# A bias put into the accumulation banks by ScalarE, and the last layer norm taken tile by tile

## The reference, cut to what matters

```python
x = layernorm(x + attention(x))          # linear attention, 32 heads of 128, gated, output projection
base   = x @ base_W.T + base_b           # 512 -> 512, the bias of 512 is what the change moves
probs  = softmax(x @ router_W.T + router_b)       # 15 routes
topk_p, topk_i = top_k(probs, 8)                  # 8 of 15; routes mapped to 8 experts
w      = sum of topk_p by expert                  # 8 weights a token
h      = x @ A.T                                  # 8 experts x rank 16
out    = base + (h * w) @ B * 2.0
x = layernorm(x + out)
```

## Time and profile before

| | us |
|---|---|
| median of 3 runs | 1011.59 (1011.27 to 1011.64) |
| the profiled execution | 1010.33 |
| its span | 1008.5 |
| TensorE busy | 994.7 (99%) |
| VectorE busy | 765.4 (76%) |
| ScalarE busy | 662.9 (66%) |
| GpSimd busy | 344.3 (34%) |

### The profile page before, as it was taken

How to read it: one execution, slowest core, us unless ns; L and a number is a source line. 1 busy time by engine, 2 the same in 40 slices (tenths; PEclk the granted TensorE clock), 3 DMA queues, 4 the chain that set the end, 5 groups by cost and what they waited for, 6 DMA issues and landing times.

```text
span 1008.5 us, 15712 instructions
## 1 busy us (share of the span) xinstructions
PE 994.7 (99%) x5620; PEld 873.8 (87%) x5620; DVE 765.4 (76%) x1102; ACT 662.9 (66%) x1108; POOL 344.3 (34%) x329
## 2 busy tenths in 40 slices
PE   8999999999999999999999999999999999999996
PEld 6878998889888898889988898888988899888886
DVE  6777875787857966778757878578677787699885
ACT  6577754787467764677647874677647786477644
POOL 1453232441443223432323414342224323321462
PEclk9999999999999999999999999999999999999999
DMA  6111121111211111111111102111111121110402
GB/s 209 34 59 57 51 70 43 50 50 30 71 43 50 50 56 49 60 50 58 53 54 58 50 30 71 42 50 51 50 50 63 40 68 51 42 51 22 147 22 84
DMA packets 48813, 57.77 MB, mean 57 GB/s; under 512 B 4320, under 2 KB 40032, under 8 KB 48736
## 3 DMA queue, kind: packets, MB, share of 16 engines
q1 hardware_dynamic: 48736, 56.77, 18.1%
HBM read 54.65 MB, written 2.10 MB: 56 GB/s over the span
## 4 chain that ended last, share of the span: by engine, by line
PE 92%; DVE 2%; ACT 2%; issue 1%; POOL 1%; DMA 1%; SPq 0%; POOLq 0%; ACTq 0%; DVEq 0%
PE ps L1834 20%; PE ps L1835 19%; PE ps L1836 19%; PE ps L1828 10%; PE ps L1829 9%; PE ps L1830 9%; PE ps L1926 2%; PE ps L1941 1%; PE ps L1928 1%; PE ps L1943 1%; DMA acc<-xt 1%; DMA stage<-stream 0%; DVE xl L1030 0%; POOL rstd L1726 0%; ACT wh L388 0%
## 5 line engine op out<-in xcount | busy, mean ns | idle before, releaser
L1834 PE MATMUL ps<-xh,wh 128*128 128x512 f32 x658 | 261.9, 398 | 0.6 <-ACT stg L436 0.6
L1835 PE MATMUL ps<-xl,wh 128*128 128x512 f32 x658 | 257.2, 391 | 0.0
L1836 PE MATMUL ps<-xh,wl 128*128 128x512 f32 x658 | 256.1, 389 | 0.0
L1743 POOL TENSOR_TENSOR stage<-stage 128x512 f32<-128x512 f32 x61 | 85.6, 1403 | 323.6 <-DMA stage<-stream 323.3
L1763 POOL TENSOR_TENSOR sqacc<-sqacc,sq 128x512 f32<-128x512 f32 x64 | 92.4, 1444 | 279.0 <-ACT sq L547 279.0
L1030 DVE TENSOR_TENSOR wl<-stage,wh 128x1024 fp32r<-128x1024 f32 (+2 forms) x145 | 155.7, 1084 | 32.6 <-ACT wh L388 32.5
L388 ACT ACTIVATE wh<-stage 128x1024 fp32r<-128x1024 f32 (+2 forms) x145 | 122.1, 855 | 55.8 <-PE ps L1830 33.7
L1836 PEld LDWEIGHTS ps<-xh,wl 128*128 128x128 f32 x658 | 123.6, 188 | 26.6
L1834 PEld LDWEIGHTS ps<-xh,wh 128*128 128x128 f32 x658 | 123.6, 188 | 24.1 <-issue 1.0
L1835 PEld LDWEIGHTS ps<-xl,wh 128*128 128x128 f32 x658 | 123.9, 188 | 22.0
L1834 PE MATMUL ps<-wh,xh 128*128 128x256 f32 (+1 forms) x416 | 121.0, 291 | 0.0
(11 more groups left out here) (201 smaller groups left out, 2193.7 us busy)
## 6 DMA issues: line engine op xcount, KB each, us to landing
stage<-stream SPq DMA_DIRECT2D x61, 384.0 KB, 3.3
stage<-stream SPq DMA_DIRECT2D x42, 256.0 KB, 2.9
stage<-stream SPq DMA_DIRECT2D x63, 128.0 KB, 2.1
dec<-decay SPq DMA_DIRECT2D x32, 192.0 KB, 2.3
acc<-xt SPq DMA_DIRECT2D x8, 256.0 KB, 6.2
v<-x SPq DMA_DIRECT2D x8, 256.0 KB, 5.6
out<-acc SPq DMA_DIRECT2D x8, 256.0 KB, 2.0
sfull<-lora_router SPq DMA_DIRECT2D x1, 512.0 KB, 4.7
```

The source lines that it names most:

```text
L1743: nc.gpsimd.tensor_tensor(stage[:, s, 1:5:3, :], stage[:, s, 0:6:5, :], stage[:, s, 7:8, :].broadcast_to([P, 2, U]), ALU.add).then_inc(t_p ...
L1834: nc.tensor.matmul(dst, wt[0], mv_[0], start=start, stop=False, skip_group_check=True)
L1835: nc.tensor.matmul(dst, wt[0], mv_[1], start=False, stop=False, skip_group_check=True)
L1836: return nc.tensor.matmul(dst, wt[1], mv_[0], start=False, stop=stop, skip_group_check=True)
```

## The change

The bias is put into seven of the eight accumulation banks by a copy on ScalarE, before the base product, whose matmuls all add onto it and are all of 400 columns. Tile 5, whose bank 6 is in use until late, keeps its opening matmul of 512 columns, and its bias is added to `acc` by GpSimd as before, once, after the weighted values of the first four tiles. The load of the bias is issued ahead of the last weights. The first columns are added right after the router's logits. The opening matmul of the second tile in each bank of the router product no longer sets the start flag. The second layer norm: tiles 5, 6 and 7 have statistics from VectorE and are normalized by it; tiles 0 to 4 go through ScalarE as before, each after the next one's square, and GpSimd makes their roots one tile at a time.

```diff
+STATS = 5
+OPENED = 5
@@ SP
-            rows_load(TAIL_LOAD + 4, 1)
             sp.wait_ge(sq_added, 2 * HEADS)
             sp.dma_start(bb, base_b.partition_broadcast(P)).then_inc(bias_in, 16)
+            rows_load(TAIL_LOAD + 4, 1)
             for t in range(TT):
-                if t < TT - 1:
+                if t < STATS:
                     sp.wait_ge(out_ready, t + 1)
                 else:
-                    sp.wait_ge(last_ready, 1)
+                    sp.wait_ge(last_ready, t - STATS + 1)
@@ ScalarE
+            def bias(t):
+                if t < 4:
+                    act.wait_ge(x1_done, t + 5)
+                elif t == 4:
+                    act.wait_ge(hw_done, 2)
+                    act.wait_ge(columns_added, 2)
+                else:
+                    act.wait_ge(ffn_read, t - 5)
+                act.wait_ge(bias_in, 16)
+                nc.scalar.activation(ps[:, FFN_BANK[t], :], bb, ACT.Copy).then_inc(bias_set, 1)
...
             variance(6)
+            bias(0)
+            bias(1)
             normalize(6, ln1_done)
             variance(7)
+            bias(2)
             transposed(5)
             normalize(7, ln1_done)
+            bias(3)
             exponent(0)
             transposed(6)
             transposed(7)
             lora_weights_hi()
+            bias(4)
             lora_transposed(0)
             exponent(1)
+            bias(6)
+            variance(TT)
             lora_transposed(1)
-            for t in range(4):
-                variance(TT + t)
-            for t in range(4):
-                normalize(TT + t, out_ready)
-            for t in range(4, 7):
-                variance(TT + t)
-            for t in range(4, 7):
-                normalize(TT + t, out_ready)
+            bias(7)
+            variance(TT + 1)
+            normalize(TT, out_ready)
+            variance(TT + 2)
+            normalize(TT + 1, out_ready)
+            variance(TT + 3)
+            normalize(TT + 2, out_ready)
+            variance(TT + 4)
+            normalize(TT + 3, out_ready)
+            normalize(TT + 4, out_ready)
@@ VectorE
             def first_columns(f):
-                dve.wait_ge(bias_added, HG * f + HG)
+                dve.wait_ge(tr_done, HG * f + HG)
+                if f == OPENED // HG:
+                    dve.wait_ge(bias_added, 1)
...
+            def statistics(t):
+                dve.wait_ge(ffn_read, t + 1)
+                link(nc.vector.bn_stats(stat[:, t - STATS, :], acc[:, t, :]))
+                nc.vector.bn_aggr(mv[:, t - STATS, :], stat[:, t - STATS, :]).then_inc(last_stats, 1)
+
+            def second_norm(t):
+                dve.wait_ge(last_rstd, 1 if t < TT - 1 else 2)
+                nc.vector.tensor_scalar(acc[:, t, :], acc[:, t, :], mv[:, t - STATS, 0:1], rstd[:, TT + t:TT + t + 1],
+                                        ALU.subtract, ALU.mult).then_inc(last_ready, 1)
...
             router_logits(0)
+            first_columns(0)
             transposed(6)
             router_top(0)
             transposed(7)
             router_weights(0)
-            first_columns(0)
...
             router_logits(1)
+            first_columns(1)
             lora_transposed(0)
             router_top(1)
             router_weights(1)
-            first_columns(1)
+            for t in range(4):
+                second_residual(t)
+                if t:
+                    second_centre(t - 1)
+            second_centre(3)
             lora_transposed(1)
+            second_residual(4)
+            second_residual(5)
+            second_centre(4)
+            statistics(5)
+            second_residual(6)
+            statistics(6)
+            second_residual(7)
+            statistics(7)
+            second_norm(5)
+            second_norm(6)
+            second_norm(7)
@@ GpSimd
-            for t in range(TT):
-                add_bias(t)
-            for n, m in ((8, 2), (10, 2), (12, 2), (14, 1)):
-                means(n, m)
-                affine(n, m)
+            def root(t, n):
+                i = t - STATS
+                pool.wait_ge(last_stats, i + n)
+                link(nc.gpsimd.tensor_scalar(mv[:, i:i + n, 1], mv[:, i:i + n, 1], EPS, None, ALU.add))
+                nc.gpsimd.tensor_tensor(rstd[:, TT + t:TT + t + n], mv[:, i:i + n, 1], half_power[:, 0:n], ALU.pow)\
+                    .then_inc(last_rstd, 1)
+            pool.wait_ge(bias_in, 16)
+            pool.wait_ge(tr_done, OPENED + 1)
+            pool.wait_ge(hw_done, 2)
+            nc.gpsimd.tensor_tensor(acc[:, OPENED, :], acc[:, OPENED, :], bb, ALU.add).then_inc(bias_added, 1)
+            for t in range(4):
+                means(TT + t)
+                affine(TT + t)
+            means(TT + 4)
+            affine(TT + 4)
+            root(5, 2)
+            root(7, 1)
@@ TensorE
             def base(t):
...
-                if t < 4:
-                    pe.wait_ge(x1_done, t + 5)
-                elif t == 4:
-                    pe.wait_ge(columns_added, 2)
-                elif t == 5:
+                if t == OPENED:
                     pe.wait_ge(ht_lo, 1)
                 else:
-                    pe.wait_ge(ffn_read, t - 5)
+                    pe.wait_ge(bias_set, t + 1 if t < OPENED else t)
                 for k in range(KT):
...
-                    if k == 0:
+                    if t == OPENED and k == 0:
                         mm3_first(...)
-                    else:
-                        mm3_onto(...)
+                        continue
+                    mm3_onto(ps[:, FFN_BANK[t], XB:W], ..., False, False)
```

More of the change, by code:

```diff
@@ L139, in build @@
         total = sb("total", [P, 2 * TT])
-        stat = sb("stat", [P, 6])
-        mv = sb("mv", [P, 2])
+        stat = sb("stat", [P, TT - STATS, 6])
+        mv = sb("mv", [P, TT - STATS, 2])
         centre = sb("centre", [P, 2 * TT])
@@ L210, in build @@
         acc_scaled, last_added, x1_done, var_done = sem("acc_scaled"), sem("last_added"), sem("x1_done"), sem("var_done")
-        affine_done, ln1_done, bias_added = sem("affine_done"), sem("ln1_done"), sem("bias_added")
+        affine_done, ln1_done, bias_set, bias_added = sem("affine_done"), sem("ln1_done"), sem("bias_set"), sem("bias_added")
         pool_step = sem("pool_step")
@@ L1611, in second_residual @@
                 dve.wait_ge(ffn_done, t + 1)
-                dve.wait_ge(bias_added, t + 1)
                 dve.wait_ge(columns_added, t // 2 + 1)
-                if t == TT - 1:
+                if t >= STATS:
                     nc.vector.tensor_tensor(acc[:, t, :], acc[:, t, :], ps[:, FFN_BANK[t], :], ALU.add)\
@@ L1675, in _ @@
             router_weights(1)
-            first_columns(1)
-            second_residual(0)
-            second_residual(1)
-            second_centre(0)
-            second_centre(1)
-            lora_transposed(1)
-            second_residual(2)
-            second_residual(3)
-            second_centre(2)
-            second_centre(3)
-            for t in range(4, TT - 1):
-                second_residual(t)
-                if t > 4:
-                    second_centre(t - 1)
-            second_centre(TT - 2)
-            second_residual(TT - 1)
-            dve.wait_ge(ffn_read, TT)
-            link(nc.vector.bn_stats(stat[:, :], acc[:, TT - 1, :]))
-            nc.vector.bn_aggr(mv[:, :], stat[:, :]).then_inc(last_stats, 1)
-            dve.wait_ge(last_rstd, 1)
-            nc.vector.tensor_scalar(acc[:, TT - 1, :], acc[:, TT - 1, :], mv[:, 0:1], rstd[:, 2 * TT - 1:2 * TT],
-                                    ALU.subtract, ALU.mult).then_inc(last_ready, 1)
+            for t in range(4):
[3 more added lines that the diff above has]
+            second_centre(3)
+            lora_transposed(1)
+            second_residual(4)
[9 more added lines that the diff above has]
+            second_norm(7)
         @block.gpsimd
@@ L1728, in affine @@
                     .then_inc(affine_done, m)
-            def add_bias(t):
-                pool.wait_ge(bias_in, 16)
-                pool.wait_ge(tr_done, t + 1)
-                nc.gpsimd.tensor_tensor(acc[:, t, :], acc[:, t, :], bb, ALU.add).then_inc(bias_added, 1)
             parts = [0]
@@ L1812, in _ @@
                 affine(t)
-            for t in range(TT):
-                add_bias(t)
-            for n, m in ((8, 2), (10, 2), (12, 2), (14, 1)):
-                means(n, m)
-                affine(n, m)
-            pool.wait_ge(last_stats, 1)
-            link(nc.gpsimd.tensor_scalar(mv[:, 1:2], mv[:, 1:2], EPS, None, ALU.add))
-            nc.gpsimd.tensor_tensor(rstd[:, 2 * TT - 1:2 * TT], mv[:, 1:2], half_power[:, 0:1], ALU.pow)\
-                .then_inc(last_rstd, 1)
+            def root(t, n):
[15 more added lines that the diff above has]
+            root(7, 1)
         @block.tensor
@@ L2220, in router_and_lora @@
                     for k in range(KT):
```

(12 more changed lines are left out.)

## The result

The changed kernel took 1006.38 us (median of 6 runs, 1005.61 to 1008.05), the kernel before beside it 1011.43 (6 runs, 1009.66 to 1012.4): a ratio of 0.9954, interval 0.9941 to 0.9967. The profiled execution took 1006.4 with a span of 1004.6.

What follows compares the result with a forecast made beforehand. TensorE is busy 99%, so only its waits and the tail count: -1.09 (gap), -0.3 (matmuls), -2.5 (tail), +0.2 (stores), +0.3 (hold) make -3.4; 1011.59 - 3.4 = 1008.2 us, range 1007.2 to 1009.8.

Steps and rivals of the forecast that it cites:

- The gap: TensorE's wait on VectorE before the first four tiles' LoRA transposes, at 982.36: closes whole, -1.09 us.
- Narrower matmuls: TensorE: seven of eight base products start with 400 columns instead of 512, taken as -0.3 us.
- The copies: ScalarE's seven bias copies into PSUM: 0.6 us each (bounds 0.5 and 0.8), no delay to TensorE.
- The thinnest slack: Tile 6's bias copy, done by 990.4, before TensorE reaches base 6 at 991.3: 0.9 us of slack.
- The bias load: Issued ahead of the last weight load, behind the LoRA-router load: taken as costing 0, bounds 0 and 0.9 us.
- Fair sharing: If loads share DMA bandwidth fairly, the earlier bias load delays ScalarE's start after the weights by 0.9 us.
- Rival B: The bias load delays the weights at 945.8 and so TensorE's first transposes: up to +0.9, 1009.1 us; chance 0.1.
- The tail: From tile 7's residual to its normalization: 2.7 us instead of 5.20, so -2.5.
- rival A: VectorE's normalizations of tiles 5 and 6 hold GpSimd's last root: last normalization 0.65 later, 1008.5 us; chance 0.2.
- C: GpSimd's additions aren't what holds the router's long operations; the gap mostly stays: gain 2.3, 1009.3 us; chance 0.1.
- D: ScalarE becomes TensorE's gate, base products wait for its copies: +1.5, 1013.1 us; chance 0.04.
- the stores: At the end, the last three outputs follow 0.55 apart while a store needs 0.65: +0.2 us, bounds 0 and 0.4.

Runs made afterwards that it cites:

- r2_hold: The changed kernel plus eight extra GpSimd additions of 512 columns, into memory nobody reads, beside the first router pass: 1008.3 us, 0.9972 of the kernel before.
- r2_wide: The changed kernel with all base products beginning with 512 columns again, zero weights in the 112: 1007.43 us, 0.9964 of the kernel before.
- r2_scalar_56: The changed kernel with tiles 5 and 6 normalized by ScalarE instead of VectorE: 1007.88 us, 0.9969 of the kernel before.
- r3_split: The changed kernel with tile 5 alone normalized by ScalarE, tiles 6 and 7 by VectorE: 1007.0 us, stretch from the mark to the end 66.47.

## Why the time fell below the range

**What held, by the prediction's own steps.**
- *The gap* closed whole. The sum starts at 972.45 (972.63 forecast), and the wait is gone. The hold by GpSimd's additions is shown both ways: taken away by the change, brought back by `r2_hold`.
- *Narrower matmuls:* 0.34 against 0.3, by `r2_wide`. With the gap, -1.41 against -1.39.
- *The copies* take 0.58 to 0.60 (0.6 forecast) and no base product waits. The thinnest slack was put at 0.9, at base 6: its bank was copied at 989.66 to 990.26, TensorE starts it at 991.15.
- *The bias load* costs 0. The Trainium skill (DMA: Bandwidth & Descriptors, on HWDGE ordering) has each DMA engine take one ring's descriptors in order, and for the weights, two loads ahead, the traces agree: they landed in 2.9 to 3.1 us with the bias load behind them and in 2.9 to 3.3 without. Fair sharing, the other end of the bound, is not what these rows show. For the 512 KB load directly ahead they don't decide: 4.3 to 5.8 us in ten traces with it, 4.3 to 4.9 in seven without. Rival B had TensorE's first transposes waiting for just these weights. They show no idle time ahead of them in either kernel, and in the changed one 0.64 of a delay would have been hidden.
- *The tail:* 2.98, where 2.7 and half a hold of 0.65 made 3.0. So rival A is half true: the hold is real, 0.19 on the first operation and 0.14 on the root, 0.35 on the path by `r2_scalar_56`. The first operation ends just after tile 5's normalization (1000.11 + 0.55 = 1000.66, and 1000.70), as A had it, and so in `r3_split` (1000.24 + 0.54 = 1000.78, and 1000.86). The root doesn't wait for tile 6's end at 1001.08 to begin its 0.58, which would give 1001.66: it ends at 1001.50. The two pages of the Trainium skill that spoke for A (GPSIMD Engine Reference, Key points; VectorE: DVE Perf Modes, Mode 2×_2P) agree as to the kind of instruction that contends; the size is the trace's.
- *Rivals B, C and D* fell. With the bias load late, ScalarE's queue did cost 1.47, but at tile 7's low half and not at the base products, as D had it.

**What failed.** First, a term: the stores. +0.2 was put for the last three leaving 0.55 apart, -0.06 came (2.51 against 2.57). They did not leave so: GpSimd's root, held as the next term of the sum allowed, made VectorE wait 0.46 ahead of tile 7, whose store left 1.01 after tile 6's and met no other. The two terms exclude each other in part, and the sum had both. The 0.67 that a store needs was sized rightly (0.65); it cost only in the two kernels that brought the stores together. The missing 0.26, with 0.02 in each of the other two sums, is the 0.3 between the sum of -3.4 and the -3.69 of the stretch. The span was forecast as 1005.1 and is 1004.6; 0.2 of this difference lies ahead of the mark. This step was mis-sized, but it alone would have left the time inside the range: 1011.59 - 3.69 = 1007.9.

Second, the step that put the number outside: "The median of the runs is 1.26 above that execution; I carry it along", with a range made only of the costs of edits. The three runs lay within 0.4 us, as if the metric had no scatter. All 74 executions of the kernel before in this study lie between 1009.42 and 1013.77, mean 1011.20, standard deviation 0.86; the 11 of the changed kernel have mean 1006.89, deviation 0.98. So of the 1.82 between 1008.2 and 1006.38, 0.3 is the sum; 0.39 is that the 1011.59 shown lay above its kernel's mean; 0.51 is that the six runs after have their median below theirs. The last 0.62 is what the means' difference (-4.31 +- 0.6) has over the stretch's 3.69; it lies inside the interval, and with the opening held the difference is -3.85 +- 0.35. By the means, and with the sum right, the forecast would have been 1011.20 - 3.69 = 1007.5. With a deviation of 0.9, a median of three executions scatters by about 0.6 and one of six by 0.45 (1.25 x 0.9 over the root of the number), their difference by 0.75. For 8 times in 10 that is 1.0 to each side; added in squares to the 1.0 that the costs had below 1008.2, the range begins at 1006.8. It would still have missed, by 0.4. With the sum right as well it begins at 1006.5, and misses by 0.1. So of the 0.8 by which the time lay below the range, a place for the scatter takes 0.4 and the right sum 0.3; the last 0.1 is chance, since a range made for 8 times in 10 is missed in 2.

That the greater part of the scatter is made in the opening is shown: waiting for the loads brings the deviation from 0.9 to 0.2 to 0.5 in the pairs (0.7 in one half's five runs). The rest, up to 0.7 us in the attention, has no cause here. Which of the first loads moves the opening was not taken apart, and the part of the 0.62 that is more than chance, if any, stays open.

## What to carry to other kernels

- Compare two traces from an instruction behind the stretch that scatters: from there each kernel's stretch repeated to 0.06 us over four traces (most of it the rounding of the span), where 18 executions with a held opening left +- 0.35 on the difference. Give the medians' own scatter a place in the range, at both ends, even if the few runs shown lie close.
- When small operations with two operands are slow beside a long operation of GpSimd, price them at what they take without it, and take GpSimd's work away rather than shorten theirs. An instruction put on an in-order engine must find its data there: the same seven copies were free with the load issued early and cost 1.47 us with it late.
- At the end of a kernel, ask when the stores leave. Making the last result 0.35 us earlier by sharing the work brought two stores together and ended 0.40 later. A hold ahead of the last result spaces the stores: don't charge both.

## What was not expected of the hardware

- GpSimd and VectorE hold each other both ways. GpSimd's remaining addition, beside VectorE's subtraction of two operands, took 1.58 us (979.00), where eight in a row took 1.256 each; its operation of one element took 0.42 and the root 0.72 beside normalizations with one SBUF tensor operand.
- A 256 KB load issued 0.5 us behind one of 512 KB landed after 5.8 us, where the larger one took 5.6. The larger one needed 0.9 more than before (4.7), but 4.3 and 4.7 occur in other traces with the same order.
- A copy of 128x512 float32 from SBUF into PSUM on ScalarE took 0.58 to 0.60 alone, 0.56 each in a pair.
